# Query weights and rows loaded in quarters, padded key rows, an earlier layer norm, and bias products in a bank fill of their own

## The reference

```python
x = x + xattn(layernorm(x), ctx)     # q = ln(x) Wq + bq, k = ctx Wk + bk, v = ctx Wv + bv; softmax(q k') v, no scale
x = x + dss(layernorm(x))            # long convolution: 512 heads, kernel of 256 steps from 64 complex states, times D
x = x + moe(layernorm(x))            # 8 experts, top 1: relu(x W1[e] + b1[e]) W2[e] + b2[e], times the gate's probability
```

## Time and profile before

| | |
|---|---|
| median of 3 runs | 419.38 us (419.14 to 419.81) |
| the profiled execution: its time, its span | 419.4 us, 417.7 us |
| mean granted clock of TensorE in it | 0.975 of full speed |
| PE, DVE, ACT, POOL busy in the span | 92%, 78%, 63%, 15% |
| bytes read by transfers | 94.08 MB, 234 GB/s over the span |
| TensorE's first product | at 11.29 us |
| TensorE's share of the chain that ended last | 87% |

### The profile page before, as it was taken

The page is one execution under the profiler, slowest core; times in us unless marked ns, Lnnn a source line. Parts: engine busy times, 40 slices in busy tenths (PEclk is TensorE's granted clock), DMA queues, the critical chain, the costliest instruction groups (busy, mean ns, idle before and its releaser), DMA issues.

```text
span 417.7 us, 5728 instructions
## 1 busy us (share of the span) xinstructions
PE 386.1 (92%) x1642; PEld 275.0 (66%) x1642; DVE 325.6 (78%) x512; ACT 261.9 (63%) x397; POOL 61.0 (15%) x63
## 2 busy tenths in 40 slices
PE   0999999999999897889999999999999999999992
PEld 0756575767984355567677676777767677676770
DVE  2778568999572886668888798898989989898880
ACT  4869588875131022258687696877878686796840
POOL 2130000000000010300040300404022040310402
PEclk9999699999999999969999999999999999999998
DMA  7999555398509900130048999989999999940100
GB/s 213 408 361 359 235 201 202 102 384 316 196 15 387 388 26 6 56 98 25 0 154 296 377 395 392 338 277 383 346 383 392 323 389 350 372 159 1 40 0 1
DMA packets 34415, 97.61 MB, mean 234 GB/s; under 512 B 2954, under 2 KB 3594, under 8 KB 32851
## 3 DMA queue, kind: packets, MB, share of 16 engines
q1 hardware_dynamic: 30322, 90.57, 58.6%
q0 software_dynamic: 2432, 6.60, 5.2%
q10 hardware_dynamic: 1632, 0.11, 0.3%
HBM read 94.08 MB, written 3.68 MB: 234 GB/s over the span
## 4 chain that ended last, share of the span: by engine, by line
PE 87%; ACT 5%; DVE 2%; DMA 2%; issue 2%; POOL 1%; SPq 0%; ACTq 0%; POOLq 0%; DVEq 0%
PE bank L1532 51%; PE bank L1356 7%; PE bank L1337 5%; PE bank L1548 4%; PE bank L1366 3%; DMA ring<-in_wq_t 2%; PE bank L1290 2%; PE bank L1345 2%; PE bank L1402 2%; ACT ring L527 1%; PE bank L1409 1%; ACT ring L520 1%; PE bank L1380 1%; PE bank L1284 1%; PE bank L1317 1%
## 5 line engine op out<-in xcount | busy, mean ns | idle before, releaser
L1176 DVE TENSOR_TENSOR w_lo<-ring,w_hi 128x1024 fp32r<-128x1024 f32 x117 | 144.7, 1263 | 27.4 <-ACT w_hi L703 26.4
L703 ACT ACTIVATE w_hi<-ring 128x1024 fp32r<-128x1024 f32 x117 | 122.0, 1053 | 47.9 <-PE bank L1532 46.9
L1532 PE MATMUL bank<-w_hi,x_hi 128*128 128x512 f32 x144 | 50.5, 433 | 3.7 <-ACT w_hi L703 3.7
L1532 PE MATMUL bank<-ring,work 128*128 128x512 f32 x108 | 49.3, 592 | 0.0
L1532 PE MATMUL bank<-w_hi,x_lo 128*128 128x512 f32 x144 | 46.4, 403 | 0.7 <-issue 0.7
L1532 PE MATMUL bank<-w_lo,x_hi 128*128 128x512 f32 x144 | 46.2, 402 | 0.0
L1532 PEld LDWEIGHTS bank<-w_hi,x_hi 128*128 128x128 f32 x144 | 27.1, 194 | 13.0 <-ACT w_hi L703 6.0
L1264 POOL TENSOR_TENSOR small<-small,x_ext 128x512 f32<-128x512 f32 x9 | 14.8, 1641 | 130.7 <-ACT small L711 130.7
L1532 PE MATMUL bank<-w_hi,h_hi 128*128 128x512 f32 x90 | 33.3, 451 | 0.0
L1532 PEld LDWEIGHTS bank<-w_hi,x_lo 128*128 128x128 f32 x144 | 27.7, 193 | 7.8 <-issue 1.2
L1532 PEld LDWEIGHTS bank<-w_lo,x_hi 128*128 128x128 f32 x144 | 27.6, 192 | 6.7
(11 more groups left out here) (193 smaller groups left out, 599.1 us busy)
## 6 DMA issues: line engine op xcount, KB each, us to landing
ring<-in_w SPq DMA_DIRECT2D x32, 2048.0 KB, 10.7
ring<-in_ctx_turned SPq DMA_DIRECT2D x4, 2048.0 KB, 12.9
ring<-in_ctx SPq DMA_DIRECT2D x4, 2048.0 KB, 15.1
x_ext<-sorted_rows POOLq DMA_DIRECT2D x9, 257.0 KB, 3.0
work<-in_b SPq DMA_DIRECT2D x8, 256.0 KB, 7.8
ring<-in_wq_t SPq DMA_DIRECT2D x1, 1024.0 KB, 9.5
x_ext<-in_x SPq DMA_DIRECT2D x1, 1024.0 KB, 11.9
x_ext<-in_bv POOLq DMA_DIRECT2D x4, 256.0 KB, 16.3
```

The source lines that it names most:

```text
L703: act.activation(w_hi[:, n % NSPLIT, :, :], weight_part(e, n), ACT.Identity).then_inc(hi_ready, 1)
L1176: dve.tensor_tensor(w_lo[:, n % NSPLIT, :, :], weight_part(e, n), w_hi[:, n % NSPLIT, :, :], ALU.subtract).then_inc(lo_ready, 1)
L1532: ins = pe.matmul(dst, kept, moved, start=start and g == 0 and q == 0, stop=stop and g == 1 and q == len(terms) - 1)
```

## The change

wq is loaded in four transfers, each of the 128 columns that one block of `wqk` reads (2048 B runs become 512 B runs), and x in four, one for each batch. Each has a semaphore of its own, and SP issues them in turn, with the tables behind them. The rows of wk are padded from 257 to 260 elements, and a product reads 258 of them. VectorE waits for each batch of x by itself in the statistics, which now come ahead of `a_phases(1)`; `a_phases(1)` stands where `a_phases(2)` stood, and `a_phases(2)` comes behind the two `xnT` copies. The bias products go into a fill `bias` of bank 3, behind the transposes on TensorE, and ScalarE copies them after its `xnT` copies. TensorE waits for the tables ahead of the transposes. The exponentials `softmax_exp(0, 0)` and `(0, 1)` go ahead of `a_magnitudes(1, 3)`.

```diff
-FILLS += [((T0, T1, T2, O_BANK)[b], ("xnT", b)) for b in range(NB)]
+FILLS += [((T0, T1, T2, O_BANK)[b], ("xnT", b)) for b in range(NB)] + [(S_BANK[3], ("bias",))]
...
+WK = DC + 4
-        wk_at = 4 * D - DCH * (DC + 1)
+        wk_at = 4 * D - DCH * WK
...
-            sp.dma_start(wq_sb, wq_t.rearrange("(e p) d -> p e d", p=P)).then_inc(qk_loaded, 16)
-            sp.dma_start(x_sb, x_rows).then_inc(x_loaded, 16)
+            def load_wq(d):
+                sp.dma_start(wq_sb[:, :, d * P:(d + 1) * P],
+                             wq_t[:, d * P:(d + 1) * P].rearrange("(e p) c -> p e c", p=P)).then_inc(wq_loaded[d], 16)
+            def load_x(b):
+                sp.dma_start(x_sb[:, b, :], x[b * P:(b + 1) * P, :]).then_inc(x_loaded[b], 16)
+            load_wq(0)
+            load_wq(1)
+            load_x(0)
+            load_x(1)
+            load_wq(2)
+            load_x(2)
+            load_x(3)
+            load_wq(3)
             sp.dma_start(tab[:], tables).then_inc(tab_loaded, 16)
...
-            after_fill(sp, ("wqk", DCH - 1))
+            after_fill(sp, ("bias",))
             sp.dma_start(wri, w_ri.rearrange("k n h -> n k h")).then_inc(wri_loaded, 16)
...  (ScalarE)
-                if d == DCH - 1:
-                    act.activation(qbias, src[:, DC + 4:DC + 7], ACT.Identity)
...
             turned_rows(1)
             turned_rows(3)
+            src = may_read(act, ("bias",))
+            did_read(act.activation(qbias, src[:, 0:3], ACT.Identity), ("bias",))
             a_sines(0)
-            after_read(act, ("wqk", DCH - 1))
+            after_read(act, ("bias",))
...
-            a_magnitudes(1, 3)
             softmax_exp(0, 0)
             softmax_exp(0, 1)
+            a_magnitudes(1, 3)
             turned_probs(0, 0)
...  (VectorE)
+                    if norms[0] == 1:
+                        dve.wait_ge(x_loaded[t], 16)
                     link(dve.bn_stats(bn6, x_sb[:, t, :]))
...
             a_phases(0)
-            a_phases(1)
-            dve.wait_ge(x_loaded, 16)
             which = norm_stats(range(NB))
             dve.wait_ge(bkq_loaded, 16)
             link(dve.tensor_tensor(bkq_prod, bkq_sb[:, :, 0], bkq_sb[:, :, 1], ALU.mult))
             dve.tensor_reduce(bkq_sum, bkq_prod, AX, ALU.add).then_inc(bkq_ready, 1)
-            a_phases(2)
+            a_phases(1)
             normalized(which, range(NB), [xn1[:, b, :] for b in range(NB)], xn1_ready)
...  (the two xnT copies of VectorE)
+            a_phases(2)
             a_phases(3)
             a_phases(4)
             a_phases(5)
-            after_read(dve, ("wqk", DCH - 1))
+            after_read(dve, ("bias",))
...  (TensorE)
-            pe.wait_ge(qk_loaded, 32)
+            pe.wait_ge(qk_loaded, 16)
             for d in range(DCH):
                 dst = may_fill(pe, ("wqk", d))
+                pe.wait_ge(wq_loaded[d], 16)
                 for e in range(DCH):
-                    ins = pe.matmul(dst[:, 0:DC + 1], wq_sb[:, e, col_slice(d)], wk_sb[:, e, :],
+                    ins = pe.matmul(dst[:, 0:DC + 2], wq_sb[:, e, col_slice(d)], wk_sb[:, e, 0:DC + 2],
                                     start=e == 0, stop=e == DCH - 1)
-                if d == DCH - 1:
...  (the wait for bkq, the bias products, the wait for the tables, the product with ones: all taken out here)
                 did_fill(ins, ("wqk", d))
+            pe.wait_ge(tab_loaded, 16)
...  (the transposes)
+            dst = may_fill(pe, ("bias",))
+            pe.wait_ge(bkq_loaded, 16)
+            for c in range(CCH):
+                for e in range(DCH):
+                    pe.matmul(dst[:, c:c + 1], wk_sb[:, e, col_slice(c)], bkq_sb[:, e, 1:2],
+                              start=e == 0, stop=e == DCH - 1)
+            pe.wait_ge(bkq_ready, 1)
+            did_fill(pe.matmul(dst[:, 2:3], ones, bkq_sum, start=True, stop=True), ("bias",))
```

More of the change, by code:

```diff
@@ L105, in perceiver_layer @@
                     w_gate, b_gate, w1, b1, w2, b2, times, tables, out):
-    x_rows = x.rearrange("(b t) h -> t b h", t=P)
     sorted_rows = nc.dram_tensor("sorted_rows", ((NB + 1) * P, D + 2), F32, kind="Internal").ap()
@@ L291, in perceiver_layer @@
         place_loaded = [sem(f"place{k}_loaded") for k in range(NSLOT)]
-        params_loaded, tab_loaded, x_loaded = sem("params_loaded"), sem("tab_loaded"), sem("x_loaded")
+        params_loaded, tab_loaded = sem("params_loaded"), sem("tab_loaded")
+        x_loaded = [sem(f"x{b}_loaded") for b in range(NB)]
         bkq_loaded = sem("bkq_loaded")
+        wq_loaded = [sem(f"wq{d}_loaded") for d in range(DCH)]
         qk_loaded, wri_loaded = sem("qk_loaded"), sem("wri_loaded")
@@ L1636 @@
         "wq_t": g["L0_xattn_Wq"].T,
-        "wkb_t": np.concatenate([g["L0_xattn_Wk"].T, g["L0_xattn_bk"][:, None]], 1),
+        "wkb_t": np.concatenate([g["L0_xattn_Wk"].T, g["L0_xattn_bk"][:, None], np.zeros((D, WK - DC - 1), np.float32)], 1),
         "bkq": np.stack([g["L0_xattn_bk"], g["L0_xattn_bq"]], 1),
```

## The result

The changed kernel takes 415.32 us (median of 6, 414.96 to 415.73), the kernel before 419.49 (median of 6); the ratio is 0.9902, with an interval of 0.9891 to 0.9914: 4.1 us faster. The forecast was 412.8, its range 411.5 to 416.3. The profiled execution took 415.35 us with a span of 413.7. The six executions lie within 0.8 us of each other. So positions are compared between profiles, and times by medians, each with its ratio to the kernel before as measured beside it.

What follows compares the result with a forecast made beforehand. Bound by wq's transfer, TensorE to 28.6 us, ScalarE to 43.05, then TensorE again; 2.9 (front) + 0.7 (idle) + 3.0 (clock) = 6.6, so 419.4 - 6.6 = 412.8 us, range 411.5 to 416.3, own range 411.6 to 414.2.

Steps and rivals of the forecast that it cites:

- The first quarter of wq lands at 8.2: Front transfers: wq's first quarter lands about a microsecond after wk at 7.0, so TensorE starts then instead of at 11.24.
- 2.9 us foreseen for the front: Front of the kernel: queries begin at 22.0 instead of 24.89, a gain of 2.9 us.
- The last batch of x lands at 14.5, between 14.1 and 16.2: Front transfers: x landed at 14.2 before; -0.7 for fewer bytes ahead and +1.0 for short packets give 14.5.
- The +1.0 for short packets: Front transfers: cost of 1536 packets of 512 B ahead of x's last batch, bounded by +0.6 and +2.7 us.
- the slower rival built on the queue's feeding: Front: SP's queue cannot feed short packets; at 128 a microsecond queries begin at 32.9, total 423.7 us; chance 0.05.
- Products end at 17.2: TensorE's first products: 32 passes take 9.01 us from 8.2, or end 1.7 us after wq's last quarter, both 17.2.
- VectorE's order, bias products over the copies: Front: statistics by batch gain 2.55 us, normalized runs 17.7 to 19.6; bias products run to 22.0 over the xnT copies.
- Exponentials first, 0.7 us, `turn_probs(0, 0)` behind `key_bias(1)`: After the scores: turn_probs(0, 0) starts at 39.4 instead of 43.05; 0.7 us of TensorE idle goes.
- The clock holds, -3.0: TensorE behind key_bias(1): clock stays at 2.4 GHz instead of falling to 1.2, 3.0 us gained, bounded by 0 and 3.0.
- The stages after it move as a block: Stages after probs_context(0): all start 6.6 us earlier, since the three engines wait for each other in the same order.
- a clock that falls at `key_bias(1)`: Rival: clock falls there anyway, gain 3.6, 415.8 us, or 414.3 if for half as long; chance 0.26.
- slow short packets: Rival at the front: short packets move at 164 GB/s, x lands 1.7 us later, 414.5 us; chance 0.12.

Runs made afterwards that it cites:

- e8: Changed kernel with GpSimd's write of the pad rows issued behind the inverse root, the late-pad-rows kernel measured a second time: 413.29 us (411.74 to 414.46).
- e6: Changed kernel with the pad rows' write issued late and wq stored by blocks in 2048 B runs: 413.4 us (0.9843).
- e4: Changed kernel with GpSimd's write of the pad rows issued behind the inverse root, first measurement: 413.65 us (411.64 to 416.73).
- e10: Changed kernel with late pad rows and VectorE's old order, a_phases(1) ahead of the statistics and a_phases(2) ahead of normalized: 414.38 us (0.9882).
- e11: Changed kernel with late pad rows and the bias products back in the last block's fill, ahead of the transposes: 415.03 us (0.9893).
- e2: Kernel before with one edit, the first two exponentials ahead of the two magnitudes: 418.44 us (0.9973).
- e1: Changed kernel with the two magnitudes put back ahead of the first exponentials: 417.3 us (0.9927).
- e5: Kernel before with only the write of the pad rows issued behind the inverse root: 418.13 us (0.9957).
- e9: Changed kernel with the magnitudes back ahead of the exponentials and four wide passes that compute nothing behind key_bias(1): 419.32 us (0.9993).
- e12: Changed kernel with late pad rows, half the bias products between query passes, and twenty passes of zeros ahead of the first product: 413.71 us (0.9844).
- e7: Changed kernel with late pad rows and half of the bias products between the first query chunk's wide passes: 412.93 us (0.9839).

## Why the prediction was right, and the step that was wrong

**The first quarter of wq lands at 8.2: wrong in this kernel.** It landed at about 11.1. The step took the queue's rate to be the same from 7 us on, and gave the waiting time of wq to its bytes. It was held by GpSimd's write of the pad rows, which no sum on SP's queue contains; with it moved (e8) the quarter landed at 8.1 and the first product started at 8.20. This is a term of the sum: 2.9 us foreseen for the front, 0.67 measured, 3.1 with the writes away.

**The last batch of x lands at 14.5, between 14.1 and 16.2:** its statistics started at 15.84 here, 1.3 late, and at 13.49 in e8. In both VectorE waited for the third batch (until 14.89 and 12.54), and the last one's statistics followed without a wait, so not the last landing bound them but the one before. The +1.0 for short packets measured 0.6 (e6), the lower bound; the upper bound, and the slower rival built on the queue's feeding, were refuted by 487 packets in a microsecond. The Trainium skill's line rate from 512 B (DMA: Bandwidth & Descriptors, Specifications) is nearer to that than my upper bound of 2.7, though not met: 0.6 us for 1536 packets.

**Products end at 17.2:** 20.57; 17.94 in e8. From a start at 8.20 the passes ran at half speed for 5.2 us there, instead of 3.6 before, though the granted column reads 1.00 as it does in the earlier trace rows. Windows of e8:

```profile
8.20:13.40 5.20, 5.20 (x12) 1.00 1.12 343
13.40:17.90 4.50, 4.50 (x23) 1.00 1.02 421
```

So the sum was 0.7 us short in e8 even with the quarter at 8.2, and the last quarter did not bind. In e4, the same kernel, the passes took 8.6 us from 8.35 on: how long the slow start lasts differs from execution to execution.

**VectorE's order, bias products over the copies:** right in direction and near in size by e10 and e11 (0.5 and 0.95 us at the queries). In the changed kernel itself they worked, but only against products that ended 3 us late.

**Exponentials first, 0.7 us, `turn_probs(0, 0)` behind `key_bias(1)`:** right; TensorE shows no idle there. It starts 1.5 us earlier and not 3.65, because the front gave so little.

**The clock holds, -3.0:** it did in the profile, and the 3.1 us are three quarters of the gain. The other five executions were not profiled; their times lie within 0.8 us and their mean granted clocks at 0.979 and 0.981, so it probably held in them too. The reason given, that the idle is gone, doesn't suffice: e2 had no idle, and the clock fell. With the magnitudes first and nothing in the gap it fell behind `key_bias(1)` in three profiles of three (before, e1, e5). With the exponentials first it fell in three of ten (e2, e4, e11) and held in seven; e4 and e8 are one kernel and differ. That fits an order that makes a fall less likely, but so few profiles don't show it. Against it stands one execution of the kernel before, measured beside e9 to e12: 415.88 us at a mean granted clock of 0.988, while the other 16 took 418.34 to 421.16 at 0.975 to 0.983. It was not profiled, so where its clock held is not known; but it seems that the kernel before can come near the changed one by the clock alone. What decides whether the clock falls is open.

**The stages after it move as a block:** nearly. From `probs_context(0)` to the end it took 362.9 us before and 363.4 now. The 0.5 us are in the experts, where TensorE waits 1.2 us instead of 0.7 for something that the profile doesn't name ("issue"); the chain after:

```profile
221.97 6.74 PE bank L1552 x22
228.71 1.25 issue
229.95 5.39 PE bank L1552 x22
```

In the other kernels that wait is between 1.0 and 1.8 (e11 has none), and in e9 and e12 over 2, where a fall of the clock follows. It doesn't grow with the gain. Between the two, the falls around the sort changed places: 3.4 and then 6.8 us before, 6.8 and then 3.4 now, with the same sum.

The time is 2.5 us off the forecast and outside the forecast's own range of 411.6 to 414.2. The errors add up: the front gave 2.2 us less than foreseen, the stages behind 0.5 less, and the order and the clock together 0.2 more. That it lies inside 411.5 to 416.3 is luck: the upper part of that range was kept for a clock that falls at `key_bias(1)` (414.3 to 415.8), which did not happen in the profile, and for slow short packets, which did not happen either. A write on another queue, for which no room was made, came out at the same number. The direction was right, and so was the size of the largest term; why the clock held stays open.

## What to carry to other kernels

Before a transfer is cut in pieces to let an engine start sooner, read the rate of all queues microsecond by microsecond up to its landing: a stretch in which busy engines move half the bytes is not paid by bytes, and another queue's write can be its cause. Where the gain of an edit lies in the granted clock, one profile proves little; take several executions of each kernel, the one before too, and count. And when a bound is removed at the front of a kernel, work out the next one: quarters, warm start and long runs each uncovered another within a microsecond.

## What the hardware showed that I had not expected

- A write of 257 KB from SBUF to memory, issued at 1.7 us, went with two microseconds (8 to 10 us) in which all queues together moved 177 GB/s (225 in the kernel before) at a busy share above 1; with the write issued later, 319 (e8).
- One queue fed 487 packets in a microsecond, most of them of 512 B (559 in e8 in the same microsecond, of all sizes).
- The same kernel, profiled twice, had the granted clock at 0.50 for 3.4 us at 21.43 and again at 41.91 in one execution, and nowhere between 13.4 and 150 us in the other (e4, e8).
- TensorE's clock rose on products of zeros: behind 20 passes of them the 32 passes took 7.1 us, and 8.6 to 10 without them (e12; e4, e7).
